# Layer 1's no-edge mask added by VectorE instead of TensorE, in a two-layer graph attention kernel, with a new order of work on every engine

## The chip, the cores and the metric

The kernel is one program on 1 core of a Trainium2 chip. The metric is the device time of that core in microseconds (us). Its engines run their own instruction streams side by side and meet only at semaphores: TensorE (PE in the profile; PEld is its weight load), VectorE (DVE), ScalarE (ACT), GpSimd (POOL), and SyncE (SP), which issues the DMAs here.

## The reference

128 graphs of 128 nodes with 256 features pass through two attention layers of 8 heads of 32.

```
# layer 0
q, k   = x@Wq + bq, x@Wk + bk                     # per head
attn   = softmax(q k^T / sqrt(32))
out    = sum over r in 0..3 of (attn * (adj == r)) @ (x@Wv[r] + bv[r])
x1     = LN(x + out@Wo + bo)
x2     = LN(x1 + gelu(x1@W1 + b1)@W2 + b2)        # W1: 256 to 1024
# layer 1
e      = q1 k1^T;  e = where(e >= 0, e, 0.2 * e)  # leaky step
attn1  = softmax(where(adj > 0, e, -9e15))
o1     = LN(attn1 @ v1)
y      = concat([o1, x2]) @ Wffn.T
result = LN(y) + x2
```

`LN` subtracts the row's mean, divides by its deviation, and (in all but name) has a gain and a shift. The changed step is the `where(adj > 0, e, -9e15)` of layer 1 together with the leaky step in front of it.

## The kernel before

The graphs are taken two at a time: 64 pairs (`G = 2`). Nothing is kept in float32 on TensorE where it can be avoided: an operand is split in two float16 parts, high and low, and a product is three matmuls (high by high, high by low, low by high). The split costs one copy on ScalarE (`..._high`, PSUM to SBUF float16) and one subtraction on VectorE (`..._low`, PSUM minus the high part). Products that need the transposed operand are preceded by TensorE transposes against an identity.

The work is software-pipelined by hand. Each engine has a function `steps(n)` that lists, in the order of its queue, what it does in step n and for which pair: `transpose_x(n)`, `attend_0(n - 1, 0)`, `scores(1, q1, k1, n - 3)`. A pair so moves through the list over five steps. There are no dynamic choices: each engine executes its list in order and waits at semaphores, which count how often a producer has finished. Once the pipeline is full, each step repeats the last exactly; "pass" means one such repeat below.

TensorE writes into the 8 banks of PSUM. The table `PE_BANKS` gives for each product of a step, in TensorE's order, its bank and which semaphore value shows that the product has been read; `bank_before` looks up the product that last used the same bank, and TensorE waits for its reader. A new order of TensorE thus comes with a new table of banks.

The steps that the prediction speaks of, in layer 0: `attend_0` (L499; matmuls at L512) multiplies the masked probabilities `pm` with the values; each half waits for `by_edge_type` on VectorE (L928, L935). `feed_forward` (L540) is 48 matmuls into bank `f`; then `residual_ff` (L1000), `attention_low_0` (L962), `normalize("f")` (L978, L983), GpSimd's `layernorm_ff` (L1163, L1165), `transpose_x2` (L547), `x2_high`, `x2_low`. From x1 come `transpose_x1` (L528), `x1_high` (L767), `x1_low` (L996), `hidden` (L533).

In layer 1: `queries_keys_1`, `values_1`, `scores` (L468), `leaky_1` (L682), `scores_max_1`, `exp_1`, `transpose_probs(1, ...)` (L490), `probs_low_1`, `attend_1` (L570), `attention_scaled_1` (L1014), GpSimd's `rstd("o1")` (L1119), `normalize("o1")`, `transpose_attention_1`, `last_product` (L586), and GpSimd's `result` (L1182, L1185).

The mask of layer 1 is made by VectorE's `no_edge` (L889): `neg_mask` is -9e15/0.2 where there is no edge and 0 elsewhere, in bfloat16. `scores` adds it by a matmul of the identity with the mask, broadcast over the two head groups, as the first product into each of the four score banks; the 16 products q k^T (32 rows by 128 columns each form, 4 row groups) accumulate on it. `leaky_1` then reads PSUM, multiplies what is negative by 0.2, and writes `p1` in SBUF.

Of the kernel before, what the change touches and what calls it, by code (L numbers as in the profile page):

```python
# [13 lines left out]
P = 128  # L14
G = 2
# [14 lines left out]
    ("pT0_0", 3, 1, "pT0_lo", 4, 1),  # L30
    ("pT0_1", 2, 1, "pT0_lo", 4, 2),
    ("xT0", 6, 0, "xT0_lo", 1, 1),
    ("pT0_2", 4, 1, "pT0_lo", 4, 3),
    ("pT0_3", 1, 1, "pT0_lo", 4, 4),
    ("v1", 0, 3, "v1_lo", 1, 1),
    ("h_0", 5, 2, "h_gelu", 4, 1),
    ("h_1", 3, 2, "h_gelu", 4, 2),
    ("edges", 4, 1, "p0_masked", 4, 4),
    ("h_2", 6, 2, "h_gelu", 4, 3),
    ("oT1", 5, 4, "oT1_affine", 1, 1),  # L40
    ("q0", 7, 0, "q0_sb", 1, 1),
    ("h_3", 5, 2, "h_gelu", 4, 4),
    ("s1_0", 6, 3, "s1_leaky", 4, 1),
    ("s1_1", 1, 3, "s1_leaky", 4, 2),
    ("s1_2", 3, 3, "s1_leaky", 4, 3),
    ("s1_3", 2, 3, "s1_leaky", 4, 4),
    ("o0_0", 5, 1, "o0_added", 2, 1),
    ("w", 7, 4, "w_normed", 1, 1),
    ("o0_1", 6, 1, "o0_added", 2, 2),
    ("f", 2, 2, "f_added", 1, 1),  # L50
    ("oT0", 4, 1, "oT0_lo", 1, 1),
    ("pT1_0", 0, 3, "pT1_lo", 4, 1),
    ("pT1_1", 1, 3, "pT1_lo", 4, 2),
    ("k0", 6, 0, "k0_sb", 1, 1),
    ("y0", 3, 1, "y0_added", 1, 1),
    ("pT1_2", 5, 3, "pT1_lo", 4, 3),
    ("pT1_3", 4, 3, "pT1_lo", 4, 4),
    ("v0_0", 7, 0, "v0_lo", 4, 1),
    ("s0_0", 3, 0, "p0_exp", 4, 1),
    ("s0_1", 1, 0, "p0_exp", 4, 2),  # L60
    ("s0_2", 0, 0, "p0_exp", 4, 3),
    ("s0_3", 6, 0, "p0_exp", 4, 4),
    ("xT1", 2, 2, "xT1_lo", 1, 1),
    ("v0_1", 4, 0, "v0_lo", 4, 2),
    ("v0_2", 5, 0, "v0_lo", 4, 3),
    ("v0_3", 7, 0, "v0_lo", 4, 4),
    ("o1_0", 2, 3, "o1_scaled", 2, 1),
    ("o1_1", 3, 3, "o1_scaled", 2, 2),
    ("k1", 1, 2, "k1_sb", 1, 1),
    ("yT0", 5, 1, "yT0_lo", 1, 1),  # L70
    ("q1", 4, 2, "q1_sb", 1, 1),
# [16 lines left out]
            "adj1_mask", "p1_max", "pT1_lo", "o1_recip", "o1_scaled", "o1_stats",  # L88
# [10 lines left out]
def build(nc, a, out):  # L99
# [12 lines left out]
    with ExitStack() as ctx:  # L112
# [259 lines left out]
        with nc.Block() as block:  # L372

            @block.sync
            def _(sp):
# [21 lines left out]
                def steps(n):  # L397
                    if live(n):
                        load_x(n)
                    if live(n - 1):  # L400
                        load_adj0(n - 1)
                    if live(n - 5):
                        store(n - 5)
                    if live(n - 1):
                        load_adj1(n - 1)
# [5 lines left out]
            def _(pe):  # L411
# [49 lines left out]
                def values_0(m, i):  # L461
                    g, cols = i // 2, slice(i % 2 * BANK, (i % 2 + 1) * BANK)
                    bank_free(f"v0_{i}", m)

                    nc.tensor.matmul(ps(f"v0_{i}")[:], ones16[:], bv_rows[:, cols], start=True, stop=False)  # L465
                    products(ps(f"v0_{i}")[:], rows_of(wv0, xT0, g, cols), first=False).then_inc(S["v0_ps"], 1)

                def scores(layer, q, k, m):  # L468
# [5 lines left out]
                    if layer == 1:  # L474
                        pe.wait_ge(S["adj1_mask"], m + 1)
                        for r in range(ROWS):
                            nc.tensor.matmul(ps(f"s1_{r}")[:], ident16[:], neg_mask[:].unsqueeze(2).broadcast_to([P, G, C, P]),
                                             start=True, stop=False)
                    for g in range(G):
                        for c in range(C):  # L480
                            at = (g * C + c) * P
                            for r in range(ROWS):
# [3 lines left out]
                                    k[rows, c, g * P:(g + 1) * P], start=(layer == 0), stop=(layer == 0 or at == 3 * P),  # L486
                                    tile_position=(r * DH, 0))
# [107 lines left out]
                def steps(n):  # L595
                    if live(n - 1):
                        transpose_probs(0, p0, n - 1, 0)
                    if live(n):
                        transpose_x(n)
                    if live(n - 1):  # L600
                        transpose_probs(0, p0, n - 1, 1)
                    if live(n - 3):
                        values_1(n - 3)
                    if live(n - 2):
                        hidden(n - 2, 0)
                        hidden(n - 2, 1)
                    if live(n - 1):
                        transpose_edges(n - 1)
                    if live(n - 2):
                        hidden(n - 2, 2)  # L610
                    if live(n - 4):
                        transpose_attention_1(n - 4)
                    if live(n):
                        queries_keys_0(n, "q0", wq0)
                    if live(n - 2):
                        hidden(n - 2, 3)
                    if live(n - 3):
                        scores(1, q1, k1, n - 3)
                    if live(n - 1):
                        attend_0(n - 1, 0)  # L620
                    if live(n - 4):
                        last_product(n - 4)
                    if live(n - 1):
                        attend_0(n - 1, 1)
                    if live(n - 2):
                        feed_forward(n - 2)
                    if live(n - 1):
                        transpose_attention_0(n - 1)
                    if live(n - 3):
                        transpose_probs(1, p1, n - 3, 0)  # L630
                    if live(n):
                        queries_keys_0(n, "k0", wk0)
                    if live(n - 1):
                        output_projection(n - 1)
                    if live(n - 3):
                        transpose_probs(1, p1, n - 3, 1)
                    if live(n):
                        values_0(n, 0)
                        scores(0, q0, k0, n)
                    if live(n - 2):  # L640
                        transpose_x2(n - 2)
                    if live(n):
                        values_0(n, 1)
                        values_0(n, 2)
                        values_0(n, 3)
                    if live(n - 3):
                        attend_1(n - 3)
                    if live(n - 2):
                        queries_keys_1(n - 2, "k1", wk1)
                    if live(n - 1):  # L650
                        transpose_x1(n - 1)
                    if live(n - 2):
                        queries_keys_1(n - 2, "q1", wq1)

                pipeline(steps, 0, 4)

            @block.scalar
            def _(act):
                copy = ACT.Copy

                def x_high(m):
                    act.wait_ge(S["xT0_ps"], m + 1)
                    if past(m):
                        act.wait_ge(S["v0_ps"], 4 * m)
                    nc.scalar.activation(flat(xT0[:, 0]), ps("xT0")[:], copy).then_inc(S["xT0_hi"], 1)
# [78 lines left out]
                def x2_high(m):  # L744
                    u = m % 2
                    act.wait_ge(S["xT1_ps"], m + 1)
                    if past(m - 1):
                        act.wait_ge(S["w_ps"], m - 1)
                        act.wait_ge(S["v1_ps"], m - 1)
                    nc.scalar.activation(flat(xT1[u][:, 0]), ps("xT1")[:], copy).then_inc(S["xT1_hi"], 1)  # L750
# [56 lines left out]
                def steps(n):  # L807
                    if live(n - 2):
                        x1_high(n - 2)
                    if live(n - 1):  # L810
                        probs_high_0(n - 1, 0)
                    if live(n):
                        x_high(n)
                    if live(n - 1):
                        probs_high_0(n - 1, 1)
                    if live(n - 3):
                        values_high_1(n - 3)
                    if live(n - 2):
                        gelu(n - 2, 0)
                        gelu(n - 2, 1)  # L820
                        hidden_high(n - 2, 0)
                    if live(n - 4):
                        attention_affine_1(n - 4)
                    if live(n - 2):
                        hidden_high(n - 2, 1)
                        gelu(n - 2, 2)
                    if live(n):
                        queries_keys_out_0(n, "q0", q0, bq_col)
                    if live(n - 2):
                        hidden_high(n - 2, 2)  # L830
                        gelu(n - 2, 3)
# [414 lines left out]
```

## Time and profile before

| | |
|---|---|
| three timed runs | 2847.48, 2848.80, 2848.91 us; median 2848.8 |
| the profiled execution | 2849.84 us |
| its span, first to last instruction | 2847.9 us |
| TensorE busy | 2697.4 us (95%), 33544 matmuls |
| VectorE busy | 2246.5 us (79%) |
| ScalarE busy | 2246.4 us (79%) |
| GpSimd busy | 1628.7 us (57%) |
| DMA queue q1, share of 16 engines | 6.2% |
| mean granted TensorE clock | 0.988 of 2.4 GHz |

Matmuls overlap, so the durations of TensorE's instructions add up to more than the time they take; how long a group holds TensorE is read from its start to the start of the next. The same holds, less strongly, for VectorE and ScalarE: an instruction listed with 0.66 us lets its successor start after 0.57 to 0.60. The idle time in brackets stands before the group, with who ended it. L numbers are lines of the kernel before.

The pipeline is full from the start of step 4 at 178.88 us to the start of step 64 at 2729.45 us: 60 passes.

### The profile page before, as it was taken

How to read it: one execution, taken by the hardware profiler on the slowest of the kernel's cores; microseconds unless marked ns; L12 is line 12 of the kernel's file. 1: busy time of each engine (PE TensorE's matmuls, PEld its weight loads, DVE VectorE, ACT ScalarE, POOL GpSimd, SP SyncE). 2: the span in 40 equal slices, each digit the busy share in tenths (PEclk: the TensorE clock that was granted, in tenths of full speed). 3: DMA queues.
4: the chain of work that ended last, by engine and by line, in shares of the span. 5: the costliest groups of instructions: out<-in, count | busy, mean ns of one | idle time of the engine just before them, and what ended most of it. 6: DMA issues, size and time to landing. Idle time of an engine off the chain costs nothing.

```text
span 2847.9 us, 86473 instructions
## 1 busy us (share of the span) xinstructions
PE 2697.4 (95%) x33544; PEld 2224.1 (78%) x33544; DVE 2246.5 (79%) x3986; ACT 2246.4 (79%) x6226; POOL 1628.7 (57%) x1870
## 2 busy tenths in 40 slices
PE   3899999999999999999999999999999999999985
PEld 2688888888878878878778788878788788888874
DVE  4588788888888887888888878878878878878863
ACT  3578878878878878878878878878878878878864
POOL 1355655655565565565565565565565565565563
PEclk9899999999999999999999999999999999999997
DMA  3000000000000000000000000000000000000000
GB/s 113 9 17 17 24 21 18 22 24 17 20 24 20 17 24 20 17 24 21 16 24 21 17 24 21 17 24 21 17 24 20 17 24 20 17 24 20 17 15 12
DMA packets 77909, 62.70 MB, mean 22 GB/s; under 512 B 6592, under 2 KB 76736, under 8 KB 77504
## 3 DMA queue, kind: packets, MB, share of 16 engines
q1 hardware_dynamic: 74336, 53.76, 6.2%
q8 instruction: 270, 4.42, 0.6%
q10 hardware_dynamic: 3168, 3.41, 0.4%
q14 instruction: 135, 1.11, 0.1%
HBM read 40.38 MB, written 16.78 MB: 20 GB/s over the span
## 4 chain that ended last, share of the span: by engine, by line
PE 55%; issue 24%; POOL 14%; DVE 4%; ACT 1%; POOLq 0%; DMA 0%; ACTq 0%
PE bank L420 40%; POOL edge_rows L1102 7%; PE bank L512 4%; PE bank L496 4%; POOL x1b L1150 3%; PE bank L484 3%; POOL oT L1169 3%; PE bank L437 3%; PE bank L465 2%; DVE o L1025 1%; DVE o_st L972 1%; DVE o_mv L976 1%; POOL o_ve L1124 0%; ACT p L705 0%; POOL o_rs L1126 0%
## 5 line engine op out<-in xcount | busy, mean ns | idle before, releaser
L935 DVE TENSOR_TENSOR pm<-pT,bank 128x4096 f16<-128x4096 f16 x256 | 568.4, 2282 | 25.8 <-issue 25.8
L420 PE MATMUL bank<-wv,xT 128*128 128x512 f16 (+1 forms) x2304 | 468.5, 344 | 0.0
L1169 POOL TENSOR_TENSOR oT<-oT_f,oT 128x512 f16<-128x512 f32 x64 | 74.4, 1163 | 606.6 <-ACT oT L805 606.6
L420 PE MATMUL bank<-yT,w 128*128 128x256 f16 x3072 | 367.1, 273 | 2.6 <-ACT oT_f L797 2.2
L705 ACT ACTIVATE p<-bank,p_nmax 128x128 f32<-128x128 f32 x1024 | 368.5, 423 | 0.0
L420 PEld LDWEIGHTS bank<-wv,xT 128*128 128x128 f16 x2304 | 226.1, 98 | 176.0 <-issue 0.3
L420 PE MATMUL bank<-w,h 128*128 128x256 f16 x3072 | 345.6, 272 | 1.7 <-POOL h L1154 1.7
L883 DVE TENSOR_TENSOR pT<-bank,pT 128x512 f16<-128x512 f32 x512 | 321.0, 675 | 10.8 <-ACT pT L779 5.8
L420 PEld LDWEIGHTS bank<-yT,w 128*128 128x128 f16 x3072 | 294.6, 98 | 40.4 <-ACT oT_f L797 2.7
L420 PEld LDWEIGHTS bank<-w,h 128*128 128x128 f16 x3072 | 295.9, 98 | 38.3 <-issue 1.9
L693 ACT ACTIVATE p<-p,p_nmax 128x128 f32<-128x128 f32 x1024 | 312.1, 390 | 0.8
L1154 POOL TENSOR_TENSOR h<-h_f,h 128x512 f16<-128x512 f32 x256 | 289.1, 1159 | 16.0 <-ACT h L680 16.0
L496 PE MATMUL bank<-ident,p 128*128 128x128 f32 x2048 | 269.2, 275 | 7.5 <-ACT p L705 4.7
L1005 DVE TENSOR_TENSOR f<-bank,x1b 128x512 f32<-128x512 f32 x64 | 44.3, 693 | 288.8 <-PE bank L420 288.8
L705 ACT ACTIVATION_READ_ACCUMULATOR p<-bank,p_nmax 128x1 f32 x1024 | 270.7, 264 | 0.0
L512 PE MATMUL bank<-v,pm 128*128 128x64 f16 (+1 forms) x8192 | 244.6, 184 | 9.9 <-issue 7.6
L512 PEld LDWEIGHTS bank<-v,pm 128*128 128x128 f16 x8192 | 235.7, 96 | 19.6 <-issue 8.1
L496 PEld LDWEIGHTS bank<-ident,p 128*128 128x128 f32 x2048 | 235.1, 143 | 10.2 <-ACT p L705 5.6
L1102 POOL TENSOR_SCALAR edge_rows<-adj_i 128x256 f16<-128x256 int32 x256 | 216.1, 861 | 39.5 <-DMA adj_i<-in_adj_dram 35.5
L883 DVE TENSOR_TENSOR v<-bank,v 128x512 f16<-128x512 f32 (+1 forms) x384 | 221.6, 591 | 11.2 <-ACT v L742 9.2
L672 ACT ACTIVATE h_f<-bank,bff_col 128x256 f32<-128x256 f32 x512 | 209.2, 481 | 1.5 <-PE bank L420 0.7
L420 PE MATMUL bank<-xT,wk 128*128 128x256 f16 x1536 | 193.4, 277 | 2.4 <-ACT p L705 2.4
(128 smaller groups left out, 5911.6 us busy)
## 6 DMA issues: line engine op xcount, KB each, us to landing
x_sb<-in_x_dram SPq DMA_DIRECT2D x64, 256.0 KB, 2.8
adj_i<-in_adj_dram SPq DMA_DIRECT2D x128, 128.0 KB, 2.7
out_dram<-out_sb SPq DMA_DIRECT2D x64, 256.0 KB, 2.1
pm<-in_L_gnn_W_dram ACTq DMA_DIRECT2D x1, 1024.0 KB, 14.0
pm<-in_L_gnn_W_dram SPq DMA_DIRECT2D x1, 1024.0 KB, 17.5
h_f<-in_L_gnn_Wffn_dram SPq DMA_DIRECT2D x1, 512.0 KB, 10.3
pm<-in_L_gnn_Wv_dram ACTq DMA_DIRECT2D x2, 256.0 KB, 10.6
pm<-in_L_gnn_Wv_dram SPq DMA_DIRECT2D x2, 256.0 KB, 11.0
```

The source lines that it names most:

```text
L420: last = nc.tensor.matmul(o, l, r, start=(first and k == 0), stop=(k == len(todo) - 1))
L437: last = nc.tensor.transpose(o[:, at:at + P], src[:, g, c * P:(c + 1) * P], ident[:])
L496: last = nc.tensor.transpose(ps(f"pT{layer}_{i}")[:, r * P:(r + 1) * P], p[:, r, g, c], ident[:])
L512: last = nc.tensor.matmul(to, pm0[g][:, s, r, hd], v, start=(r == 0 and s == 0), stop=(r == REL - 1 and s == 0))
L672: last = nc.scalar.activation(h_f[:, c], ps(f"h_{i}")[:, (c % 2) * T:(c % 2 + 1) * T], ACT.Gelu, bias=bff_col[:, c:c + 1])
L693: last = nc.scalar.activation(p1[:, r, g, c], p1[:, r, g, c], ACT.Exp, bias=p1_nmax[:, r, g, c:c + 1])
L705: last = nc.scalar.activation(p0[:, r, g, c], ps(f"s0_{r}")[:, at:at + P], ACT.Exp, bias=p0_nmax[:, r, g, c:c + 1], accum_out=p0_sum[:, g, ...
L883: return V_.tensor_tensor(to, source, high, ALU.subtract)
L935: V_.tensor_tensor(pm0[g][:, s], pT0[g][:, s].unsqueeze(1).broadcast_to([P, REL, HEADS, P]), edges[:, g].unsqueeze(2).broadcast_to([P, REL ...
L1102: last = V_.tensor_scalar(edge_rows[:, :, r], adj0_i[:], float(r), None, ALU.is_equal)
L1154: V_.tensor_tensor(h[:, 1, 2 * i:2 * i + 2], h_f[:, 2 * i:2 * i + 2], h[:, 0, 2 * i:2 * i + 2], ALU.subtract).then_inc(S["h_lo"], 1)
L1169: V_.tensor_tensor(oT1[:, 1], oT1_f[:], oT1[:, 0], ALU.subtract).then_inc(S["oT1_lo"], 1)
```

## The change

Four things are changed.

First, `scores(1, ...)` on TensorE has no mask products; each of its 16 q k^T products starts its own region of the bank.

Second, VectorE has a new function `mask_scores_1`: four additions, one for each score bank, of the 512 scores in PSUM and the broadcast `neg_mask` in SBUF, into `p1`. It waits for the scores, the mask, and (as `leaky_1` did) for the transposes of the previous pair's probabilities. The score banks are released by it, not by `leaky_1`.

Third, `leaky_1` on ScalarE works in place in `p1`, from SBUF to SBUF.

Fourth, the `steps` lists of all five engines and `PE_BANKS` are written in another order. Steps begin elsewhere in the same cycle (what was step n is now spread over the end of one step and the start of the next, and the lists run one step further), and within the cycle jobs are moved. Since layer 0's queries, keys and values are no longer followed by all that had implied their order, some waits are added: `values_0` waits for `xT0_lo`, `x_high` for `q0_ps` and `k0_ps`, `x2_high` for `q1_ps` and `k1_ps`; `no_edge` waits for `s1_masked` in place of `s1_ps`.

```diff
                 def scores(layer, q, k, m):
...
-                    if layer == 1:
-                        pe.wait_ge(S["adj1_mask"], m + 1)
-                        for r in range(ROWS):
-                            nc.tensor.matmul(ps(f"s1_{r}")[:], ident16[:], neg_mask[:].unsqueeze(2).broadcast_to([P, G, C, P]),
-                                             start=True, stop=False)
...
                 def leaky_1(m, r):
-                    act.wait_ge(S["s1_ps"], m + 1)
-                    if past(m):
-                        act.wait_ge(S["pT1_ps"], 4 * m)
-                    nc.scalar.activation(p1[:, r].rearrange("p g c j -> p (g c j)"), ps(f"s1_{r}")[:], ACT.Prelu,
-                                         alpha=ALPHA).then_inc(S["s1_leaky"], 1)
+                    act.wait_ge(S["s1_masked"], 4 * m + r + 1)
+                    nc.scalar.activation(p1[:, r], p1[:, r], ACT.Prelu, alpha=ALPHA).then_inc(S["s1_leaky"], 1)
...
+                def mask_scores_1(m):
+                    dve.wait_ge(S["s1_ps"], m + 1)
+                    dve.wait_ge(S["adj1_mask"], m + 1)
+                    if past(m):
+                        dve.wait_ge(S["pT1_ps"], 4 * m)
+                    for r in range(ROWS):
+                        V_.tensor_tensor(p1[:, r], ps(f"s1_{r}")[:].rearrange("p (g c j) -> p g c j", g=G, c=C),
+                                         neg_mask[:].unsqueeze(2).broadcast_to([P, G, C, P]), ALU.add).then_inc(S["s1_masked"], 1)
...
-    ("s1_0", 6, 3, "s1_leaky", 4, 1),
+    ("s1_0", 7, 4, "s1_masked", 4, 1),
...
-                pipeline(steps, 0, 4)
+                pipeline(steps, 0, 5)
```

The new order is shown at three places. The first is TensorE's queue from the feed-forward product (`w,h`) on: `ident,o` is `transpose_attention_0`, `ident,p` the transposes of layer 1's probabilities (4 matmuls each), `wo,oT` the output projection, `k,q` layer 0's scores, `ident,x_0` or `ident,x_1` `transpose_x2`. Before:

```order
L420 MATMUL bank<-w,h 128x256 x48
L437 MATMUL bank<-ident,o 128x128 x4
L496 MATMUL bank<-ident,p 128x128 x8
L420 MATMUL bank<-xT,wk 128x256 x12
L420 MATMUL bank<-wo,oT 128x256 x12
L496 MATMUL bank<-ident,p 128x128 x8
L465 MATMUL bank<-bv_rows,ones 128x512
L420 MATMUL bank<-wv,xT 128x512 x6
L484 MATMUL bank<-k,q 128x128 x16
L437 MATMUL bank<-ident,x_0 128x128 x4
L465 MATMUL bank<-bv_rows,ones 128x512
L420 MATMUL bank<-wv,xT 128x512 x6
```

Now:

```order
L419 MATMUL bank<-w,h 128x256 x48
L436 MATMUL bank<-ident,o 128x128 x4
L490 MATMUL bank<-ident,p 128x128 x16
L419 MATMUL bank<-wo,oT 128x256 x12
L465 MATMUL bank<-bv_rows,ones 128x512
L419 MATMUL bank<-wv,xT 128x512 x6
L479 MATMUL bank<-k,q 128x128 x16
L465 MATMUL bank<-bv_rows,ones 128x512
L419 MATMUL bank<-wv,xT 128x512 x6
L436 MATMUL bank<-ident,x_1 128x128 x4
L465 MATMUL bank<-bv_rows,ones 128x512
L419 MATMUL bank<-wv,xT 128x512 x6
```

Between the feed-forward product and `wo,oT` there stood the query/key product `xT,wk` and 12 transposes in all; now there are 20 transposes and no product. Two value products (`wv,xT`) stand between the output projection and `transpose_x2`, where there was one.

The second is VectorE's queue from the normalise of o1 (`o<-o,o_mv,o_rs`) to the products by edge type (`pm`). Before:

```order
L983 TENSOR_SCALAR o<-o,o_mv,o_rs 128x256 x2
L883 TENSOR_TENSOR v<-bank,v 128x16x32
L883 TENSOR_TENSOR yT<-bank,yT 128x512
L883 TENSOR_TENSOR pT_0<-bank,pT_0 128x512 x2
L883 TENSOR_TENSOR pT_1<-bank,pT_1 128x512 x2
L883 TENSOR_TENSOR xT<-bank,xT 128x512
L883 TENSOR_TENSOR v<-bank,v 128x8x32 x2
L935 TENSOR_TENSOR pm_0<-pT_0,bank 128x4096 x2
L935 TENSOR_TENSOR pm_1<-pT_1,bank 128x4096 x2
```

Now, from one row before that normalise (`yT` is `x1_low`, `p<-bank,neg_mask` the new additions):

```order
L879 TENSOR_TENSOR yT<-bank,yT 128x512
L988 TENSOR_SCALAR o<-o,o_mv,o_rs 128x256 x2
L879 TENSOR_TENSOR v<-bank,v 128x8x32 x2
L879 TENSOR_TENSOR pT_0<-bank,pT_0 128x512 x2
L879 TENSOR_TENSOR xT<-bank,xT 128x512
L879 TENSOR_TENSOR pT_1<-bank,pT_1 128x512 x2
L879 TENSOR_TENSOR v<-bank,v 128x16x32
L940 TENSOR_TENSOR pm_0<-pT_0,bank 128x4096 x2
L898 TENSOR_TENSOR p<-bank,neg_mask 128x512 x4
L940 TENSOR_TENSOR pm_1<-pT_1,bank 128x4096 x2
```

`x1_low` was behind the normalise of o1 and is now in front of it. Nine subtractions stood between that normalise and the products by edge type, and eight stand there now (`x1_low` has gone to the front). The four additions of the mask stand between the two halves of the products.

The third is GpSimd's queue after the statistics of o1 (`o_ve`, `o_rs`). Before:

```order
L1124 TENSOR_SCALAR o_ve<-o_mv 128x2
L1126 TENSOR_TENSOR o_rs<-o_ve,minus_half 128x2
L1150 TENSOR_TENSOR x1b<-x,b_row 128x512
L1102 TENSOR_SCALAR edge_rows<-adj_i 128x2x128 x4
L1169 TENSOR_TENSOR oT<-oT_f,oT 128x512
```

Now:

```order
L1133 TENSOR_SCALAR o_ve<-o_mv 128x2
L1135 TENSOR_TENSOR o_rs<-o_ve,minus_half 128x2
L1191 TENSOR_TENSOR out_sb<-w_n,g2b_row 128x512
L1194 TENSOR_TENSOR out_sb<-out_sb,x2b 128x512
L1126 TENSOR_TENSOR xbo<-x_sb,bo_row 128x512
L1111 TENSOR_SCALAR edge_rows<-adj_i 128x2x128 x4
L1163 TENSOR_TENSOR h<-h_f,h 128x512
```

Behind `o_rs` there stood one addition for x1 and then the edge-type comparisons; now the two instructions of `result` and the addition for the next pair's residual stand there.

On SyncE, `load_adj0(n)` now stands in front of `load_x(n)`, and `load_adj1` is issued for pair n - 3 in step n.

## Rows read from the trace of the kernel before

**Rows 1.** Busy time by stretch, one pass; us, busy (x count), PEclk, DMA share, GB/s:

```profile
1409.84:1452.34 42.50, 41.72 (x524) 34.52 (x525) 34.92 (x64) 34.84 (x99) 25.39 (x29) 1.00 0.07 21
```

**Rows 2.** Waits of TensorE from 178.88 to 2729.45 us: total, times, longest:

```profile
PE bank L420 <- POOL oT L1169: 29.4, 60, 0.8
PE bank L437 <- POOL x L1144: 18.1, 60, 0.3
```

**Rows 3.** Timeline, TensorE: start us, duration us, engine, line, operation, count, [idle before]:

```profile
1422.55 1.03 PE L477 MATMUL bank<-neg_mask,ident 128*128 128x512 bf16 x4
...
1423.50 1.17 PE L484 MATMUL bank<-k,q 32*128 32x128 f32 x32
...
1424.61 1.91 PE L512 MATMUL bank<-v,pm 128*128 128x64 f16 x64
...
1427.00 0.82 PE L420 MATMUL bank<-wffn,oT 128*128 128x256 f16 x6 [0.48 <-POOL oT L1169]
...
1429.62 1.90 PE L512 MATMUL bank<-v,pm 128*128 128x64 f16 x64
...
1436.71 0.60 PE L437 MATMUL bank<-ident,o 128*128 128x128 f32 x4
...
1437.15 1.04 PE L496 MATMUL bank<-ident,p 128*128 128x128 f32 x8
...
1438.02 1.47 PE L420 MATMUL bank<-xT,wk 128*128 128x256 f16 x12
...
1439.44 1.47 PE L420 MATMUL bank<-wo,oT 128*128 128x256 f16 x12
```

**Rows 4.** Timeline, VectorE, from the end of the feed-forward product:

```profile
1436.91 0.69 DVE L1005 TENSOR_TENSOR f<-bank,x1b 128x512 f32<-128x512 f32 x1 [4.52 <-PE bank L420]
...
1438.64 0.66 DVE L883 TENSOR_TENSOR oT<-bank,oT 128x512 f16<-128x512 f32 x1
1439.21 1.28 DVE L883 TENSOR_TENSOR pT<-bank,pT 128x512 f16<-128x512 f32 x2
1440.41 0.73 DVE L983 TENSOR_SCALAR f<-f,f_mv,f_rs 128x256 f32<-128x256 f32 x2
```

**Rows 5.** Timeline, GpSimd, layer 0's second norm:

```profile
1441.22 1.27 POOL L1163 TENSOR_TENSOR x<-f,g_row 128x512 f32<-128x512 f32 x1 [0.85 <-DVE f L983]
1442.57 1.27 POOL L1165 TENSOR_TENSOR x<-x,beta_row 128x512 f32<-128x512 f32 x1
```

**Rows 6.** Timeline, TensorE, from the transposes of x2:

```profile
1401.83 0.66 PE L437 MATMUL bank<-ident,x 128*128 128x128 f32 x4
...
1405.35 0.38 PE L465 MATMUL bank<-bv_rows,ones 128*128 128x512 f16 x1
...
1406.86 1.37 PE L420 MATMUL bank<-v,pT 128*128 128x33 f16 x48
...
1408.07 1.47 PE L420 MATMUL bank<-xT,wk 128*128 128x256 f16 x12
...
1410.31 1.47 PE L420 MATMUL bank<-xT,wq 128*128 128x256 f16 x12
...
1411.62 1.04 PE L496 MATMUL bank<-ident,p 128*128 128x128 f32 x8
```

**Rows 7.** Timeline, ScalarE, the copy after those transposes:

```profile
1402.52 0.60 ACT L750 ACTIVATE xT<-bank 128x512 f16<-128x512 f32 x1 [2.55 <-PE bank L437]
```

**Rows 8.** Timeline, GpSimd, around the o1 statistics:

```profile
1410.41 0.22 POOL L1124 TENSOR_SCALAR o_ve<-o_mv 128x2 f32<-128x2 f32 x1 [0.72 <-DVE o_mv L976]
...
1411.39 1.27 POOL L1150 TENSOR_TENSOR x1b<-x,b_row 128x512 f32<-128x512 f32 x1
```

**Rows 9.** Timeline, VectorE, the o1 normalise and the masked products:

```profile
1411.46 1.76 DVE L983 TENSOR_SCALAR o<-o,o_mv,o_rs 128x256 f32<-128x256 f32 x2 [1.24 <-POOL o_rs L1126]
...
1413.13 0.68 DVE L883 TENSOR_TENSOR v<-bank,v 128x512 f16<-128x512 f32 x1
...
1418.44 8.88 DVE L935 TENSOR_TENSOR pm<-pT,bank 128x4096 f16<-128x4096 f16 x4 [0.38 <-issue]
```

More of the change, by code:

```diff
@@ new lines @@
+    ("pT0_3", 7, 2, "pT0_lo", 4, 4),
+    ("h_0", 0, 3, "h_gelu", 4, 1),
+    ("h_1", 6, 3, "h_gelu", 4, 2),
+    ("oT1", 4, 5, "oT1_affine", 1, 1),
+    ("edges", 2, 2, "p0_masked", 4, 4),
+    ("k1", 3, 4, "k1_sb", 1, 1),
+    ("h_2", 5, 3, "h_gelu", 4, 3),
+    ("s1_0", 7, 4, "s1_masked", 4, 1),
+    ("s1_1", 0, 4, "s1_masked", 4, 2),
+    ("s1_2", 1, 4, "s1_masked", 4, 3),
+    ("s1_3", 3, 4, "s1_masked", 4, 4),
+    ("h_3", 5, 3, "h_gelu", 4, 4),
+    ("o0_0", 4, 2, "o0_added", 2, 1),
+    ("q0", 5, 1, "q0_sb", 1, 1),
@@ new lines @@
+    ("k0", 0, 1, "k0_sb", 1, 1),
+    ("w", 7, 5, "w_normed", 1, 1),
+    ("o0_1", 3, 2, "o0_added", 2, 2),
+    ("f", 5, 3, "f_added", 1, 1),
+    ("oT0", 0, 2, "oT0_lo", 1, 1),
+    ("pT1_0", 3, 4, "pT1_lo", 4, 1),
+    ("pT1_1", 6, 4, "pT1_lo", 4, 2),
+    ("pT1_2", 1, 4, "pT1_lo", 4, 3),
+    ("pT1_3", 4, 4, "pT1_lo", 4, 4),
+    ("y0", 0, 2, "y0_added", 1, 1),
+    ("v0_0", 5, 1, "v0_lo", 4, 1),
+    ("s0_0", 1, 1, "p0_exp", 4, 1),
+    ("s0_1", 7, 1, "p0_exp", 4, 2),
+    ("s0_2", 3, 1, "p0_exp", 4, 3),
@@ L72 @@
+    ("s0_3", 4, 1, "p0_exp", 4, 4),
+    ("v0_1", 2, 1, "v0_lo", 4, 2),
+    ("xT1", 6, 3, "xT1_lo", 1, 1),
+    ("v0_2", 0, 1, "v0_lo", 4, 3),
+    ("v1", 6, 3, "v1_lo", 1, 1),
+    ("o1_0", 2, 4, "o1_scaled", 2, 1),
+    ("o1_1", 5, 4, "o1_scaled", 2, 2),
+    ("q1", 7, 3, "q1_sb", 1, 1),
+    ("v0_3", 1, 1, "v0_lo", 4, 4),
+    ("yT0", 5, 2, "yT0_lo", 1, 1),
+    ("xT0", 2, 0, "xT0_lo", 1, 1),
+    ("pT0_0", 4, 1, "pT0_lo", 4, 1),
+    ("pT0_1", 3, 1, "pT0_lo", 4, 2),
 ]
@@ L485, in scores @@
                                     ps(f"s{layer}_{r}")[:, at:at + P], q[rows, c, g * P:(g + 1) * P],
-                                    k[rows, c, g * P:(g + 1) * P], start=(layer == 0), stop=(layer == 0 or at == 3 * P),
-                                    tile_position=(r * DH, 0))
+                                    k[rows, c, g * P:(g + 1) * P], start=True, stop=True, tile_position=(r * DH, 0))
                     last.then_inc(S[f"s{layer}_ps"], 1)
@@ new lines, in steps @@
+                    if live(n - 4):
+                        queries_keys_1(n - 4, "k1", wk1)
+                    if live(n - 3):
+                        hidden(n - 3, 2)
+                    if live(n - 4):
+                        scores(1, q1, k1, n - 4)
+                    if live(n - 3):
+                        hidden(n - 3, 3)
+                    if live(n - 2):
+                        attend_0(n - 2, 0)
+                    if live(n - 1):
+                        queries_keys_0(n - 1, "q0", wq0)
+                        queries_keys_0(n - 1, "k0", wk0)
@@ new lines, in steps @@
+                    if live(n - 5):
+                        last_product(n - 5)
+                    if live(n - 2):
+                        attend_0(n - 2, 1)
+                    if live(n - 3):
+                        feed_forward(n - 3)
+                    if live(n - 2):
+                        transpose_attention_0(n - 2)
+                    if live(n - 4):
+                        transpose_probs(1, p1, n - 4, 0)
+                        transpose_probs(1, p1, n - 4, 1)
+                    if live(n - 2):
+                        output_projection(n - 2)
@@ new lines, in steps @@
+                    if live(n - 1):
+                        values_0(n - 1, 0)
+                        scores(0, q0, k0, n - 1)
+                        values_0(n - 1, 1)
+                    if live(n - 3):
+                        transpose_x2(n - 3)
+                    if live(n - 1):
+                        values_0(n - 1, 2)
+                    if live(n - 3):
+                        values_1(n - 3)
+                    if live(n - 4):
+                        attend_1(n - 4)
+                    if live(n - 3):
+                        queries_keys_1(n - 3, "q1", wq1)
@@ new lines, in steps @@
+                    if live(n - 3):
+                        gelu(n - 3, 1)
+                        gelu(n - 3, 2)
+                    if live(n - 5):
+                        attention_affine_1(n - 5)
+                    if live(n - 3):
+                        gelu(n - 3, 3)
+                    if live(n - 5):
+                        attention_high_1(n - 5)
+                    if live(n - 3):
+                        hidden_high(n - 3, 1)
+                    if live(n - 4):
+                        leaky_1(n - 4, 0)
@@ L875, in _ @@
-                pipeline(steps, 0, 4)
+                pipeline(steps, 0, 5)
             @block.vector
@@ L1086, in _ @@
-                pipeline(steps, 0, 4)
+                pipeline(steps, 0, 5)
             @block.gpsimd
@@ L1212, in steps @@
[L1212 to L1220 removed]
+                    if live(n - 3):
+                        hidden_low(n - 3, 0)
+                    if live(n - 5):
+                        attention_low_1(n - 5)
+                    if live(n - 3):
+                        hidden_low(n - 3, 1)
+                        residual_bias_ff(n - 3)
+                        hidden_low(n - 3, 2)
+                        hidden_low(n - 3, 3)
@@ new lines, in steps @@
+                    if live(n - 5):
+                        rstd("w", n - 5)
+                    if live(n - 2):
+                        attention_scaled_0(n - 2)
+                    if live(n - 5):
+                        shift_w(n - 5)
+                        residual_shift_1(n - 5)
+                    if live(n - 3):
+                        rstd("f", n - 3)
+                        layernorm_ff(n - 3)
+                    if live(n - 2):
+                        rstd("y0", n - 2)
+                        layernorm_0(n - 2)
@@ L1224 @@
+                    if live(n - 4):
+                        rstd("o1", n - 4)
+                    if live(n - 5):
+                        result(n - 5)
+                    if live(n):
+                        residual_bias_0(n)
+                pipeline(steps, 0, 5)
 _INS = ["x", "adj", "L0_gnn_Wq", "L0_gnn_bq", "L0_gnn_Wk", "L0_gnn_bk", "L0_gnn_Wv", "L0_gnn_bv", "L0_gnn_Wo", "L0_gnn_bo",
```

368 lines of the change are left out of this document (128 added, 240 removed).

## The prediction

> **What bounds the kernel now.** The table of busy time by stretch comes first: in one pass of 42.50 us TensorE is busy for 41.72, VectorE for 34.92, ScalarE for 34.84, GpSimd for 25.39, at a granted clock of 1.00, the level of 2.4 GHz [rows 1]. TensorE is nearly full, so next the list of its waits over the 60 full passes: it waits for GpSimd's low part of the attention (29.4 us, 0.49 a pass) and for x1 (18.1 us, 0.30 a pass), and for nothing else of size [rows 2]. Of 42.50 us some 0.8 are such waits. Then the timelines of each engine over one pass, for how long each group holds its engine (start to next start).
>
> The reader should take from this that a pass ends when TensorE has come round, but that the others are not idle by much. If TensorE's list shortens, the pass is set by whichever ring of dependences through VectorE, ScalarE and GpSimd is longest in the new order.
>
> **What leaves TensorE.** The four mask products hold it from 1422.55 to 1423.50, 0.95 us a pass [rows 3]. With no wait changed, 60 x 0.95 = 57 us would go. The score products behind them stay, 1.11 us.
>
> **What comes to VectorE.** Four additions of 512 elements, one operand in PSUM and one in SBUF. The nearest rows are the addition of the same form into f, 0.69 us for one, and the subtractions, of which two let the next start after 1.20 us, 0.60 each [rows 4]. So 2.4 to 2.8 us a pass; I take 2.4. VectorE's load becomes 34.9 + 2.4 = 37.3 us, still under the pass, so what counts is what is queued behind the additions: the second half of the products by edge type, and behind that the maxima, for which layer 1's exponentials wait. The leaky step reads SBUF, not PSUM, 4 times; a ScalarE copy of this size takes 0.60 [rows 7], and even at 0.1 more each it has room, since the exponentials wait for the maxima. I cost it at nothing, at most 0.4.
>
> The Trainium skill ("VectorE: DVE Perf Modes", "Why PSUM operands drop a tier") says that an operand in PSUM keeps a float32 instruction at one element a cycle; that agrees with these rows and would give the same 0.6 to 0.7, so it does not decide.
>
> **The new order, as one ring.** I put the clock at F = 0 where TensorE leaves the feed-forward product, the row at 1436.71, and follow what must happen until the next F.
>
> 1. VectorE adds f at 0.20 and starts the low part of the attention at 1.93, as the rows 1436.91 and 1438.64 stand behind 1436.71 [rows 3, 4]. The output projection started at 1439.44, that is at 2.73. In the new order only 20 transposes stand before it, 0.44 + 2 x 0.87 = 2.18 us [rows 3]: TensorE waits 0.55 us there (the query/key product that covered this is gone).
> 2. VectorE now does all four subtractions of layer 1's probabilities at once: 1.93 + 0.57 + 4 x 0.60 = 4.90, where normalising f starts. GpSimd starts 0.81 later (1441.22 behind 1440.41) and has x2 ready after 1.35 + 1.27 = 2.62, at 8.33 [rows 4, 5]. TensorE starts 0.14 after a releaser's end, as 1439.44 stands behind VectorE's 1438.64 + 0.66. So the transposes of x2 start at 8.47. TensorE alone would be there at 2.73 + 1.31 + 1.51 + 1.11 + 1.51 = 8.17; it waits up to 0.3 us.
> 3. x2 transposed is copied 0.69 us after the start of the transposes, 0.60 long [rows 6, 7]; the subtraction takes 0.66, and two handovers 0.03 + 0.14: `values_1` can start at 8.47 + 2.12 = 10.6. Then `values_1` 1.31, `attend_1` 1.21, the queries 1.31, the last value product 1.51 (the distances of the rows in group 6): x1 is transposed at 15.9.
> 4. Its copy and subtraction, as in 3, but only until VectorE can start its next instruction: 0.69 + 0.60 + 0.03 + 0.57 = 1.89. At 17.8 VectorE comes to the normalise of o1.
> 5. This normalise is the hinge. The two took 1.67 us (1411.46 to 1413.13), though the same form on f takes 0.64 to the next start (1440.41, 0.73 long for two) [rows 4, 9]. GpSimd had started a float32 addition 0.07 us before (1411.39), and the first normalise ended only behind it [rows 8, 9]. It costs nothing now, since the path had room. In the new order GpSimd's statistics of o1 start 3.55 us behind `attend_1` (1410.41 behind 1406.86) and its next large instruction 4.53 behind it (1411.39), at 11.9 + 4.53 = 16.4; that is now the first of `result`, the second follows 1.35 later, at 17.8 [rows 5, 6, 8]. VectorE comes at 17.8 too. It meets either this second instruction or, had it come earlier, the first; behind them a third stands ready. I take the collision as before, counted from GpSimd's start: 17.8 + (1413.13 - 1411.39 = 1.74) = 19.5.
> 6. Then 8 subtractions, six of 512 elements at 0.60 and two of 256, which I count like the two normalises of f, 0.64 together [rows 4]: 4.24, so the products by edge type start at 23.8. Their first half takes 8.88 / 2 = 4.44, then 0.14: `attend_0` can start at 28.4. TensorE alone: x1's subtraction ends at 17.9, frees the bank of the transposes of the probabilities at 18.1, then 0.87 + 0.44 + 0.45 + 5 x 1.31 + 1.11 = 9.4 gives 27.5. So it waits about 0.9 us here. (Of the 0.9 some 0.2 is taken earlier, at the edge transposes, whose bank waits for x's subtraction.)
> 7. From there TensorE has no wait: 1.91 for half the attention, 2 x 1.31 for queries and keys, 2.62 for the last product, 7.09 for the other half and the feed-forward, = 14.24 [rows 3, 6]. The next F is at 28.4 + 14.2 = 42.6. The second half of the attention starts at 28.4 + 7.15 = 35.5 and needs the second half of the products: 23.8 + 4.4 + 2.4 + 4.44 + 0.14 = 35.2. That leaves 0.3 us: the additions of the mask may cost 0.68 each before they count. GpSimd's low parts and the exponentials have 1 to 3 us of room.
>
> Pass before 42.50, after 42.6: 42.63 by the unrounded terms, so +0.13 x 60 = +8 us. As a cross-check: the old waits (0.79) and the mask products (0.95) go, and waits of 0.55, 0.3, 0.15 (step 3, where TensorE alone would take 0.49 + 1.51 of the 2.12) and 0.9 come: 42.50 - 1.74 + 1.9 = 42.66. Outside the 60 passes the masks' products go (4 x 0.95) and the additions lengthen the drain (4 x 0.7 at each of few places); I take nothing, 4 us either way. New loads of x and adj on SyncE are asked for at least a third of a pass before use and the DMA engines are busy for 0.07 of the pass [rows 1]; nothing. The profiled execution took 2849.8 us; 2849.8 + 8 = 2858. The median of the runs lies 1.0 lower: 2857 us.
>
> The Trainium skill ("SBUF — State Buffer", "Who interferes with whom") says that VectorE in a two-port mode and GpSimd take a shared pair of ports as a lock, for a whole instruction, whoever issues first; by that rule the additions of the mask, with one operand in SBUF, are not held up, and the normalise is. The trace agrees for the normalise: 1.76 against 0.73 us for the pair [rows 4, 9].
>
> **Rivals.**
>
> *VectorE comes first at the hinge.* The two meet within 0.05 us by my count, which has an error of 0.1 to 0.2. If the normalise gets in before `result`'s second instruction and takes 0.64, step 6 ends at 27.3, under TensorE's 27.5. The pass is then 18.1 + 9.4 + 14.2 = 41.7: -0.8 x 60 = -47 us, 2801 us. For it: the tie, and that the second normalise of the pair was not held up by the comparisons started 0.1 us before it. Against: where the trace has them meet, GpSimd's lead was 0.07 us and enough, and GpSimd is busy without a gap from 16.4 to 20.2. This rival ends on the other side; the point from which it decides is a lead of VectorE of about 0.05 us at L983 over L1185.
>
> *A further wait.* The ring holds for sure only what I listed. A wait that I missed, additions of 0.8 us each or more, or the second normalise caught by GpSimd's third instruction (1.3 us more), adds 0.4 to 1.3 a pass: 2880 to 2930 us. For it: 0.3 us of room at step 7 and 0.8 at x1. Against: the pure load of no other engine is near.
>
> *The waits don't come.* TensorE's own list is 42.50 - 0.79 - 0.95 = 40.8 us. Were it full, 2849.8 - 1.7 x 60 gives 2746. Against it: steps 1 and 2 rest on distances that VectorE and GpSimd kept in every pass.
>
> **How the numbers follow.** The forecast's ring 0.48, VectorE first 0.30, a further wait 0.14, fewer waits than both 0.08. The likeliest case by itself spans 42.4 to 42.9 a pass, 2843 to 2873 us. The range reaches over VectorE first (2801, down to 2795) and into the further wait: 2795 to 2882; about 0.1 is left out on each side. A change under 0.2% (5.7 us, 0.1 us a pass) can't be told from none. Of the forecast's 0.48, 0.10 lies below that, 0.14 within, 0.24 above. Faster: 0.30 + 0.08 + 0.10 = 0.48; same 0.14; slower 0.24 + 0.14 = 0.38. So the single likeliest time is a little slower, while the chance of faster is larger than that of slower, because all the other outcomes of weight but one lie there.
>
> **What would show it.** TensorE's list of waits should name VectorE's low part at the output projection (0.5 us a pass), GpSimd's x2 (0.2 to 0.3) and, largest, the wait of `attend_0` (0.7 to 0.9) for the products by edge type. The normalise of o1 should have a mean of about 0.9 us; at 0.41 the first rival holds. The additions of the mask should last 0.66 to 0.70 us. The prediction is wrong in its ring if TensorE waits elsewhere for more than 0.5 us a pass, and wrong in its hinge if the normalise is short and the pass near 41.7.

## The result and the profile after

The changed kernel takes 2893.3 us (median of 6 runs, 2891.2 to 2894.5), the kernel before 2848.0 on the same chip. The ratio is 1.0157, 95% interval 1.0144 to 1.0171: slower by 1.6%, outside the predicted range of 2795 to 2882 us. The profiled execution's span is 2889.7 us. One execution of e3 ran at a mean granted clock of 0.655 and took 3810.2 us; it is left out of every number here.

One full pass, from TensorE's end of one feed-forward product to the next; it answers to [rows 1], columns as there:

```profile
1405.86:1449.02 43.16, 41.31 (x522) 33.82 (x521) 37.70 (x66) 34.83 (x97) 25.35 (x30) 1.00 0.07 20
```

The pass is 43.16 us where it was 42.50. TensorE is busy for less and VectorE for 2.8 us more, but neither is full. Of 59 full passes 55 are like this one and four are shorter, 42.20 to 42.24 (they are read further down, at the first rival); the mean is 43.11, so that some 60 x 0.60 = 36 of the span's 42 us more lie in the full passes and the rest in filling and draining. TensorE's waits between 230 and 2700 us (total, times, longest), which answer to [rows 2]:

```profile
PE bank L419 <- DVE v L879: 42.9, 54, 0.9
PE bank L506 <- issue: 26.7, 57, 0.5
PE bank L419 <- DVE oT L879: 22.0, 57, 0.5
PE bank L490 <- DVE yT L879: 11.0, 57, 0.2
```

The two old waits are gone. Four new ones stand in nearly every pass: 0.80 for VectorE's low part of v1, whose bank the second product of `hidden` needs (bank 6 in `PE_BANKS`), 0.47 in front of `attend_0` (its releaser is not named; VectorE's first half of the masked products ends 0.10 us before), 0.38 for the attention's low part, 0.19 for x1's. Together 1.84 us, counted from the end of the matmul in front. TensorE in one pass; the clock F = 0 of the prediction is at 1405.86 [rows 3, 6]:

```profile
1405.86 0.60 PE L436 MATMUL bank<-ident,o 128*128 128x128 f32 x4
...
1408.59 1.47 PE L419 MATMUL bank<-wo,oT 128*128 128x256 f16 x12 [0.38 <-DVE oT L879]
...
1414.31 0.63 PE L436 MATMUL bank<-ident,x 128*128 128x128 f32 x4
...
1421.78 0.60 PE L436 MATMUL bank<-ident,x 128*128 128x128 f32 x4
...
1423.88 1.07 PE L490 MATMUL bank<-ident,p 128*128 128x128 f32 x8 [0.19 <-DVE yT L879]
...
1427.06 1.48 PE L419 MATMUL bank<-yT,w 128*128 128x256 f16 x12 [0.80 <-DVE v L879]
...
1435.08 1.90 PE L506 MATMUL bank<-v,pm 128*128 128x64 f16 x64 [0.47 <-issue]
...
1442.05 1.90 PE L506 MATMUL bank<-v,pm 128*128 128x64 f16 x64
...
1449.02 0.60 PE L436 MATMUL bank<-ident,o 128*128 128x128 f32 x4
```

The output projection starts at F + 2.73, x2's transposes at 8.45, x1's at 15.92, the first half of `attend_0` at 29.22, the next F at 43.16. VectorE in the same pass [rows 4, 9]:

```profile
1407.78 0.66 DVE L879 TENSOR_TENSOR oT<-bank,oT 128x512 f16<-128x512 f32 x1
...
1410.75 0.72 DVE L988 TENSOR_SCALAR f<-f,f_mv,f_rs 128x256 f32<-128x256 f32 x2
...
1423.66 2.68 DVE L988 TENSOR_SCALAR o<-o,o_mv,o_rs 128x256 f32<-128x256 f32 x2
1426.25 0.74 DVE L879 TENSOR_TENSOR v<-bank,v 128x256 f16<-128x256 f32 x2
...
1430.51 4.47 DVE L940 TENSOR_TENSOR pm<-pT,bank 128x4096 f16<-128x4096 f16 x2
1434.90 2.47 DVE L898 TENSOR_TENSOR p<-bank,neg_mask 128x512 f32<-128x512 f32 x4
```

and its second normalise of o1 alone:

```profile
1424.98 1.36 DVE L988 TENSOR_SCALAR o<-o,o_mv,o_rs 128x256 f32<-128x256 f32 x1
```

GpSimd [rows 5, 8]:

```profile
1411.55 1.27 POOL L1172 TENSOR_TENSOR x<-f,g_row 128x512 f32<-128x512 f32 x1 [2.48 <-DVE f L988]
...
1422.28 1.27 POOL L1191 TENSOR_TENSOR out_sb<-w_n,g2b_row 128x512 f32<-128x512 f32 x1
1423.63 1.27 POOL L1194 TENSOR_TENSOR out_sb<-out_sb,x2b 128x512 f32<-128x512 f32 x1
1424.86 1.32 POOL L1126 TENSOR_TENSOR xbo<-x_sb,bo_row 128x512 f32<-128x512 f32 x1
```

This is the place to read. GpSimd starts `result`'s second instruction (L1194) at 1423.63, VectorE the first normalise at 1423.66. The normalise lasts until just behind that instruction. GpSimd has by then started the addition for the next residual (L1126, 1424.86), and the second normalise (1424.98) lasts 1.36 us, until 0.16 behind that one. From the first normalise to VectorE's next instruction 2.59 us pass, where the prediction had 1.7 and the unhindered pair of f takes 0.64 (1410.75 to 1411.39). Over the whole kernel, mean duration of one in ns (the prediction had about 900 for the normalise):

```profile
L988 DVE TENSOR_SCALAR o<-o,o_mv,o_rs 128x256 f32<-128x256 f32 x128 | 164.6, 1326 | 2.3 <-POOL o_rs L1135 2.3
...
L898 DVE TENSOR_TENSOR p<-bank,neg_mask 128x512 f32<-128x512 f32 x256 | 158.1, 673 | 11.1 <-PE bank L479 11.1
```

The Trainium skill ("SBUF — State Buffer", "Who interferes with whom") has the loser of the shared ports wait for the other's whole instruction. The trace agrees in part. Each of the two normalises is held by a GpSimd instruction that had started first, and ends 0.16 us behind the listed end of that instruction. Since a normalise needs 0.41 us itself, it was let in about 0.25 us before that end (an estimate from these rows; spans on GpSimd are rough). The comparisons of the kernel before, which had also started first, held a normalise for far less than their length (lines at e4), so there the measurement departs from the rule. What the trace adds is that GpSimd's next instruction got its turn between two normalises that stood back to back.

### The profile page after: what moved, and what is told of

It reads as the page before. It is cut to its first block and busy times, and to the rows that moved or that the text cites. A ratio compares the mean times of both kernels' runs of the same rounds, so it can differ in the third digit from the quotient of the medians.

```text
span 2889.7 us, 86408 instructions
## 1 busy us (share of the span) xinstructions
PE 2667.5 (92%) x33288; PEld 2175.6 (75%) x33288; DVE 2422.2 (84%) x4242; ACT 2245.0 (78%) x6226; POOL 1626.9 (56%) x1870
## 5 line engine op out<-in xcount | busy, mean ns | idle before, releaser
L419 PE MATMUL bank<-yT,w 128*128 128x256 f16 x3072 | 377.3, 273 | 48.1 <-DVE v L879 45.6
L734 ACT ACTIVATE v<-bank 128x512 f16<-128x512 f32 x256 | 159.8, 624 | 248.6 <-PE bank L419 248.6
L490 PE MATMUL bank<-ident,p 128*128 128x128 f32 x2048 | 257.9, 274 | 17.9 <-DVE yT L879 12.9
L490 PEld LDWEIGHTS bank<-ident,p 128*128 128x128 f32 x2048 | 227.7, 142 | 31.7 <-issue 26.0
L879 DVE TENSOR_TENSOR v<-bank,v 128x512 f16<-128x512 f32 (+1 forms) x384 | 215.7, 589 | 0.4 <-ACT v L757 0.3
L419 PE MATMUL bank<-xT,wq 128*128 128x256 f16 x1536 | 190.9, 275 | 3.3 <-ACT p L697 1.9
```

The source lines that it names most:

```text
L419: last = nc.tensor.matmul(o, l, r, start=(first and k == 0), stop=(k == len(todo) - 1))
L490: last = nc.tensor.transpose(ps(f"pT{layer}_{i}")[:, r * P:(r + 1) * P], p[:, r, g, c], ident[:])
L734: nc.scalar.activation(value_part(i, 0), by_head(ps(f"v0_{i}")), copy).then_inc(S["v0_hi"], 1)
L879: return V_.tensor_tensor(to, source, high, ALU.subtract)
```

## The experiments

All were compared with the kernel before on the same chip. Theory 1: the pass is set by the ring of the prediction, lengthened because both normalises are held up. Rival: VectorE's additions and load, or another of TensorE's waits, set it.

**e1, both GpSimd jobs away from the normalise.**

```diff
+                    if live(n - 1):
+                        residual_bias_0(n - 1)     # behind hidden_low(n - 3, 0)
...
                         rstd("y0", n - 2)
+                    if live(n - 5):
+                        result(n - 5)
+                    if live(n - 2):
                         layernorm_0(n - 2)
                     if live(n - 4):
                         rstd("o1", n - 4)
-                    if live(n - 5):
-                        result(n - 5)
-                    if live(n):
-                        residual_bias_0(n)
```

> New order with one change: GpSimd does result between rstd(y0) and layernorm_0 (a gap of 3.1 us in the changed kernel's trace), and residual_bias_0 one step later behind hidden_low 0, so that nothing large runs on GpSimd when VectorE comes to the normalise of o1. Theory 1 (both normalises are held up by GpSimd's float32 instructions under way, 2.59 us instead of 0.64, and this is the ring that sets the pass of 43.16): the pair takes 0.64 to 0.73, attend_0 no longer waits for the products by edge type, pass 41.7 to 41.8, about 2810 us. Rival (the additions of the mask and VectorE's load of 37 us set the pass, or TensorE's other waits do): pass 43.0 to 43.2, 2885 to 2893 us.

Measured: 2791.2 us, ratio 0.9805 (0.979 to 0.982) to before. Faster than both kernels, and further than expected. The pass:

```profile
1403.22:1444.74 41.52, 40.93 (x523) 33.99 (x522) 35.83 (x66) 34.77 (x97) 25.34 (x30) 1.00 0.08 22
```

VectorE's normalise pair, and its successor after 0.64 us:

```profile
1421.01 0.73 DVE L988 TENSOR_SCALAR o<-o,o_mv,o_rs 128x256 f32<-128x256 f32 x2
1421.65 0.75 DVE L879 TENSOR_TENSOR v<-bank,v 128x256 f16<-128x256 f32 x2
```

TensorE waits only for these (230 to 2640 us):

```profile
PE bank L419 <- DVE oT L879: 22.5, 58, 0.6
PE bank L490 <- DVE yT L879: 11.3, 58, 0.2
```

The 0.80 and 0.47 us are gone with the 1.95 us that the normalises had been held. Moving two jobs on an engine that is 56% busy took 102 us from the changed kernel.

**e2, one of the two away.** The edit is e1's first and last part: `residual_bias_0` alone is moved.

> New order with residual_bias_0 alone moved (behind hidden_low 0, one step later); result stays where it meets the normalise of o1. Theory 1: the first normalise still waits for result's second instruction, the second no longer waits: 1.7 us for the pair, pass 43.16 - 0.9 = 42.25, about 2838 us; this is the single collision that the prediction had reckoned with. Rival (load of VectorE or another wait): 2885 to 2893 us.

Measured: 2839.0 us, ratio 0.997 (0.996 to 0.998), pass 42.21. The pair lasts nearly as long as in the kernel before, 1.72 us against 1.76:

```profile
1443.18 1.72 DVE L988 TENSOR_SCALAR o<-o,o_mv,o_rs 128x256 f32<-128x256 f32 x2
```

with GpSimd 0.02 us ahead:

```profile
1443.16 1.27 POOL L1194 TENSOR_TENSOR out_sb<-out_sb,x2b 128x512 f32<-128x512 f32 x1
```

This is the single collision of the prediction. The 0.80 us in front of `hidden` is gone from TensorE's list, the 0.47 in front of `attend_0` stays. The collision that went away had cost 43.16 - 42.21 = 0.95 us a pass. The one that is left costs 42.21 - 41.52 = 0.69 against e1, although it holds the pair for 1.0 us: the other 0.3 TensorE would have needed anyway.

**e3, the other away.** The edit is e1's second part: `result` alone is moved, so `residual_bias_0` stays behind `rstd("o1")`.

> New order with result alone moved to between rstd(y0) and layernorm_0; residual_bias_0 then follows rstd(o1) and runs at about 1422.3 to 1423.6, where VectorE comes to the normalise at 1423.66. Theory 1: GpSimd's instruction has just ended, so the normalises are short, pass 41.7 to 41.9, about 2812 us; should VectorE come 0.1 us earlier, the first normalise is caught for a remainder of 0.1 to 0.2 only. Rival (load or another wait): 2885 to 2893 us.

Measured: 2792.6 us, ratio 0.9806 (0.979 to 0.982). GpSimd's addition and the normalise pass each other:

```profile
1421.89 1.27 POOL L1126 TENSOR_TENSOR xbo<-x_sb,bo_row 128x512 f32<-128x512 f32 x1
```

```profile
1423.26 0.73 DVE L988 TENSOR_SCALAR o<-o,o_mv,o_rs 128x256 f32<-128x256 f32 x2
```

The addition ended at 1423.16, VectorE came at 1423.26, and the pair lasts 0.73. The same instruction is in the way in the changed kernel and harmless 0.10 us past its end: the moment decides, not GpSimd's load.

**e4, a GpSimd instruction of another form in the way.** The kernel leaves out layer 0's output bias.

```diff
-                    V_.tensor_tensor(xbo[u][:], x_sb[u][:], both(bo_row), ALU.add).then_inc(S["x_plus_bo"], 1)
+                    V_.tensor_scalar(xbo[u][:], x_sb[u][:], 1.0, None, ALU.mult).then_inc(S["x_plus_bo"], 1)
```

> New order, everything in place, but residual_bias_0 is a tensor_scalar with one input tensor (times 1.0) instead of the addition of two tensors; it leaves out layer 0's output bias. It tells why before's second normalise passed the comparisons that had started 0.1 us ahead of it. If what matters is that GpSimd's instruction reads one tensor, the second normalise passes: 1.7 us for the pair, pass near 42.25, about 2838 us. If any float32 instruction of 512 elements that GpSimd has under way holds VectorE, the pair stays at 2.4 to 2.6 us and the time at about 2893 us (less what the one-input form is shorter).

Measured: 2860.8 us, ratio 1.0048 (1.003 to 1.006), pass 42.57: between the two. GpSimd:

```profile
1411.30 1.27 POOL L1194 TENSOR_TENSOR out_sb<-out_sb,x2b 128x512 f32<-128x512 f32 x1
1412.65 1.51 POOL L1126 TENSOR_SCALAR xbo<-x_sb 128x512 f32<-128x512 f32 x1
```

The second normalise:

```profile
1412.64 0.77 DVE L988 TENSOR_SCALAR o<-o,o_mv,o_rs 128x256 f32<-128x256 f32 x1
```

It lasts 0.77 us, against 1.36 behind the two-input addition and 0.48 behind the comparisons of before, while the one-input instruction itself is longer (1.51). It also started 0.01 us behind the normalise, not 0.12 ahead of it as the addition did, so this run doesn't separate the form from the lead. Before against after does at nearly one lead. In the kernel before, GpSimd's comparisons and the second normalise:

```profile
1412.63 3.44 POOL L1102 TENSOR_SCALAR edge_rows<-adj_i 128x256 f16<-128x256 int32 x4
```

```profile
1412.73 0.48 DVE L983 TENSOR_SCALAR o<-o,o_mv,o_rs 128x256 f32<-128x256 f32 x1
```

The comparisons were 0.10 us ahead and cost 0.07, the addition 0.12 ahead and cost 0.95. The two differ in type, shape and operation as well as in the number of inputs; which of these is the reason is not shown.

**e5, the mask back on TensorE in the new order.** `mask_scores_1` is taken out; the four mask products and `leaky_1` are as before, and the bank table names `s1_leaky`. ScalarE's four leaky steps now stand in one piece, in front of the attention's first half:

```diff
+                    if layer == 1:
+                        pe.wait_ge(S["adj1_mask"], m + 1)
+                        for r in range(ROWS):
+                            nc.tensor.matmul(ps(f"s1_{r}")[:], ident16[:], neg_mask[:].unsqueeze(2).broadcast_to([P, G, C, P]),
+                                             start=True, stop=False)
```

> New order, but the mask is added by TensorE again (the four mask products in front of layer 1's scores, leaky step out of PSUM, the four leaky steps in one piece so that the banks come free in time). Theory: the late normalise of o1 still sets when attend_0 can start; of the 0.95 us that the mask products need, 0.47 fit in TensorE's wait in front of attend_0, 0.48 do not: pass 43.16 + 0.48 = 43.6, about 2920 us. Rival (VectorE's additions are what slowed the changed kernel): without them the pass falls to 42.5 or below, 2850 us or less.

Measured: 2911.6 us, ratio 1.0223 (1.021 to 1.024), pass 43.52 (forecast 43.6). The wait in front of `attend_0` is gone and the others are as in the changed kernel:

```profile
PE bank L419 <- DVE v L887: 42.6, 53, 0.9
PE bank L419 <- DVE oT L887: 21.9, 57, 0.5
PE bank L496 <- DVE yT L887: 11.0, 57, 0.2
```

The rival falls: without VectorE's additions the kernel is slower still, by 18 us. In the new order, with the late normalise, moving the mask gained 0.36 us a pass, about a third of its 57 us.

**e6, the mask moved in the old order.** The mask's code is that of the change; the order and the banks are those of before. The additions stand behind the second half of the products by edge type:

```diff
                         by_edge_type(n - 1, 1)
+                    if live(n - 3):
+                        mask_scores_1(n - 3)
+                    if live(n - 1):
                         recip_0(n - 1)
```

> Order and banks of before, with the mask alone moved: VectorE adds it behind the second half of the products by edge type. Theory: before, TensorE waits 0.49 us a pass for layer 1's attention (GpSimd's low part), which hangs on a chain through ScalarE that is busy from layer 0's exponentials on; the mask products lie in front of that wait, so their 0.95 us turns into a longer wait of about 1.4 us and the pass stays at 42.5, with 0 to 0.4 for the additions: 2848 to 2870 us. Rival (TensorE's list sets the pass): 42.50 - 0.95 = 41.55, about 2791 us.

Measured: 2851.2 us, ratio 1.001 (1.000 to 1.002), pass 42.49. TensorE's waits:

```profile
PE bank L420 <- POOL oT L1172: 39.0, 58, 0.9
PE bank L506 <- ACT h_f L666: 35.6, 58, 0.6
PE bank L437 <- POOL x L1147: 17.3, 58, 0.3
```

The wait for GpSimd's low part went from 0.49 to 0.67 a pass and a new one of 0.61 stands in front of `attend_0`, whose bank ScalarE's gelu still has to read. The mask products had been cover for a chain of ScalarE; taken out alone they gave back nothing.

**e7, e1 with the mask on TensorE.** The edits of e1 and e5 together.

> As e1 (new order, GpSimd quiet at the normalise of o1), but the mask added by TensorE as in e5. Theory: in e1 TensorE waits only 0.57 us a pass (0.38 in front of the output projection, 0.19 in front of the transposes of the probabilities) and both lie elsewhere in its list, so the mask products cost their full 0.95: 41.52 + 0.95 = 42.47, about 2848 us. Rival (VectorE's 2.4 us of additions cost e1 something too): less than that, 42.0 or below, under 2820 us.

Measured: 2845.7 us, ratio 0.9995 (0.9986 to 1.0004), pass 42.46 (forecast 42.47), and the waits of e1:

```profile
PE bank L419 <- DVE oT L887: 22.2, 58, 0.6
PE bank L496 <- DVE yT L887: 11.2, 58, 0.2
```

So with the normalise out of the way the moved mask is worth 2845.7 - 2791.2 = 54.5 us, 0.94 a pass: all that the four products took, and VectorE's additions cost nothing that can be seen.

**e8, an attempt to get below e1.**

```diff
                         probs_low_1(n - 4, 0)
-                        probs_low_1(n - 4, 1)
                     if live(n - 3):
                         normalize("f", lambda g: f[:, g], lambda g: f[:, g], n - 3)
+                    if live(n - 4):
+                        probs_low_1(n - 4, 1)
```

> As e1, with VectorE's normalise of f placed after two of the four subtractions of layer 1's probabilities, as it stood before. The transposes of x2 then need not wait (0.18 us in e1's trace). Theory: those 0.18 us go only in part, since VectorE's subtraction of x2 behind the maxima comes next: 41.52 - 0.05 to 0.15, 2782 to 2788 us. Rival (the waits up to x2 don't matter, because the output projection's wait sets the rest): no change, 2791 us.

Measured: 2803.5 us, ratio 0.9841 (0.983 to 0.986), pass 41.70; both theories missed. x2 is in time now, but TensorE waits earlier, at layer 0's scores, whose last bank is that of layer 1's last transposes; VectorE reads it 0.64 us later. x2's transposes start at F + 8.61, 0.16 later than in e1, for want of nothing but that:

```profile
1416.95 1.17 PE L479 MATMUL bank<-k,q 32*128 32x128 f32 x32 [0.27 <-issue]
...
1419.58 0.60 PE L436 MATMUL bank<-ident,x 128*128 128x128 f32 x4
```

```profile
1415.31 1.28 DVE L879 TENSOR_TENSOR pT<-bank,pT 128x512 f16<-128x512 f32 x2
1416.51 0.68 DVE L997 TENSOR_TENSOR y<-bank,xbo 128x512 f32<-128x512 f32 x1
```

A bank's reader is a dependence as good as the data. e1 stays the fastest kernel here.

## Why the prediction was wrong, step by step

**Bound and removal.** Right: the ring of dependences, not TensorE's load, sets the pass (e1 and e2 shorten it by 1.64 and 0.95 us without a change to TensorE's instructions). The runs split the change from 42.50 to 43.16 into four parts: the new order alone -0.04 (e7), the mask moved -0.94 (e1 against e7), one collision +0.69 (e2 against e1), the other +0.95.

**The additions.** Right: 673 ns for one, the four within 2.47 us, and no cost (e7).

**Steps 1 to 4.** The starts were right to 0.03 us: 2.73, 8.47, 15.9 and 17.8 were forecast; 2.73, 8.45, 15.92 and 17.80 came. The wait at the output projection is listed with 0.38 and not 0.55, because the list counts from the end of the last transpose (1406.30 + 1.91), the prediction from where the next matmul could have started; the start itself was as forecast. For the same reason the wait for x2 is in no list.

**Step 5 failed.** The arrivals of GpSimd and VectorE were right (both at F + 17.8, in that order by 0.03 us). But the prediction carried the price of the collision over from before, 1.74 us from GpSimd's start, as if one normalise of the pair could be caught. That price is right where GpSimd's next instruction is a comparison (the kernel before) or none (e2, 1.66 us). With the addition there, both were caught: 2.62 us from GpSimd's start. Taking one away (e2) gave 2839.0, both (e1) 2791.2. The wait of 0.80 us in front of `hidden`, by its size what the prediction called a sign that its ring was wrong, is this second collision's: it is gone in e2. The prediction named a second catch as part of its second rival, with 2880 to 2930 us, and gave that 0.14: too little, since its own argument said that GpSimd was busy without a gap.

**Steps 6 and 7.** The subtractions (4.26, forecast 4.24) were right. From `attend_0` to the next F it was 13.94, not 14.24: each half holds TensorE for 1.73 us here, and the prediction had 1.91 and 1.86. So 42.63 + 0.88 - 0.30 gives 43.2, and 43.16 was measured. With the one collision that it had reckoned with, the pass is 42.21 and not 42.63 (e2, 2839 us and not 2857): the forecast owes part of its nearness to two errors of opposite sign, 0.95 too little for the second collision and 0.42 too much elsewhere.

**The first rival**, VectorE first, was the one with 0.30. VectorE came 0.03 us late for it, but a small lead would not have given its pass of 41.7 either. In the four short passes of the changed kernel GpSimd came about 0.3 us later than usual. The first normalise ran in 0.40 us, and the second met `result`'s second instruction:

```profile
734.22 1.27 POOL L1194 TENSOR_TENSOR out_sb<-out_sb,x2b 128x512 f32<-128x512 f32 x1
```

```profile
733.92 1.71 DVE L988 TENSOR_SCALAR o<-o,o_mv,o_rs 128x256 f32<-128x256 f32 x2
```

That is one collision again, and a pass of 42.2. A pass of 41.5 came only with GpSimd's work moved away (e1, e3). The rival had priced the pair as if VectorE had only to win the first meeting; it was the same omission as in step 5.

**Two small slips**, on which nothing hangs: the value product in front of layer 0's scores holds TensorE for 1.6 us and not 1.51, so that TensorE alone would reach x2's transposes at 8.26; and the third rival's time is 2745 us by its own terms, not 2746.

## What to carry over

Follow the ring in absolute times, engine by engine; here that gave the first four steps to a few hundredths of a us. Where VectorE's SBUF-to-SBUF instruction meets a busy GpSimd, price it once for each instruction that can be caught, and look at what GpSimd runs next. Here the cure was to move GpSimd's free work, not to speed anything up. Work taken off the fullest engine pays only if the wait that it covered doesn't come back (e6), and a new order can lose at one meeting of two engines more than it gained: here 1.64 us a pass against 0.98.

## What the runs showed that was not expected

Two normalises back to back on VectorE are not one claim: GpSimd's addition, started 0.12 us ahead of the second, held it for 0.95 us, though it had come behind the first. And GpSimd's comparisons, 0.10 us ahead of the second normalise in the kernel before, held it for only 0.07.
